# First attention of a two-layer kernel: scores from queries and keys of 64 channels, two heads side by side, stages of four heads

## The reference, cut to what matters

```python
H, D = 16, 64                                   # 8 batches, 256 queries, 1601 keys, 128 channels
q = (x @ Wq).reshape(B, S, H, D).transpose(0, 2, 1, 3)      # x: layer-normed tokens
k = (c @ Wk).reshape(B, N, D, H).transpose(0, 3, 2, 1)
v = (c @ Wv).reshape(B, N, D, H).transpose(0, 3, 1, 2)
mask = jnp.all(c == 0, axis=-1)[:, None, None, :]
scores = jnp.where(mask, -jnp.inf, jnp.einsum('bhsd,bhdn->bhsn', q, k) * D ** -0.5)
out = jnp.einsum('bhsn,bhnd->bhsd', jax.nn.softmax(scores, axis=-1), v)
return out.transpose(0, 2, 1, 3).reshape(B, S, H * D) @ Wo
```

## Time and profile before

| | |
|---|---|
| median of 3 runs | 2098.92 us (2096.93 to 2101.98) |
| profiled execution: time, span | 2103.45 us, 2101.7 us |
| PE busy, share of the span | 1975.8 us, 94% |
| DVE busy | 1674.0 us, 80% |
| ACT busy | 1071.4 us, 51% |
| POOL busy | 1196.0 us, 57% |
| first attention | from 0 to about 1576 us |

### The profile page before, as it was taken

The page is one execution under the profiler, slowest core; times in us unless marked ns, Lnnn a source line. Parts: engine busy times, 40 slices in busy tenths (PEclk is TensorE's granted clock), DMA queues, the critical chain, the costliest instruction groups (busy, mean ns, idle before and its releaser), DMA issues. The chain is left out here.

```text
span 2101.7 us, 35280 instructions
## 1 busy us (share of the span) xinstructions
PE 1975.8 (94%) x10757; PEld 1446.0 (69%) x10757; DVE 1674.0 (80%) x4067; ACT 1071.4 (51%) x1509; POOL 1196.0 (57%) x655
## 2 busy tenths in 40 slices
PE   7999999999999999999999999999987799769995
PEld 5667776777677777767777777777655588557774
DVE  7898888878788888888788888888656677757755
ACT  4444545354454545353544545454546699644442
POOL 5556575757466665757575665657666355223340
PEclk8999999999999999999999999999998999879997
DMA  3000000000000000000000000000000212112300
GB/s 97 1 8 10 2 3 17 1 1 4 18 1 4 17 1 1 3 18 1 4 1 17 1 4 6 1 1 1 6 1 21 82 64 77 37 47 63 87 24 24
DMA packets 56401, 40.81 MB, mean 19 GB/s; under 512 B 2516, under 2 KB 53660, under 8 KB 55196
## 3 DMA queue, kind: packets, MB, share of 16 engines
q1 hardware_dynamic: 56220, 38.57, 6.2%
HBM read 37.45 MB, written 1.11 MB: 18 GB/s over the span
## 5 line engine op out<-in xcount | busy, mean ns | idle before, releaser
L580 POOL TENSOR_TENSOR a_den<-a_den,a_probs 128x1024 f32<-128x1024 f32 x352 | 845.0, 2402 | 353.8 <-ACT a_probs L823 353.3
L823 ACT ACTIVATE a_probs<-a_probs,a_mask_col 128x1024 f32<-128x1024 f32 x416 | 478.9, 1151 | 576.6 <-DVE a_probs L1058 576.3
L1058 DVE TENSOR_TENSOR a_probs<-a_scores,a_shift 128x512 f32<-128x512 f32 x832 | 565.7, 686 | 150.5 <-PE a_scores L611 128.2
L957 DVE CUSTOM_DVE_ANT_0 a_work<-a_work,a_mask_row 128x400 f32<-128x400 f32 (+1 forms) x1024 | 572.5, 590 | 47.7 <-PE a_work L643 47.5
L711 PE MATMUL a_pv<-a_probs,a_V 128*64 128x256 f32 x3328 | 405.2, 385 | 0.9 <-ACT a_probs L823 0.9
L609 PE MATMUL a_scores<-a_Q_hi,a_cT_hi 128*128 128x512 f32 x832 | 346.0, 416 | 5.9 <-DVE a_probs L1058 4.4
L610 PE MATMUL a_scores<-a_Q_lo,a_cT_hi 128*128 128x512 f32 x832 | 328.5, 395 | 0.0
L643 PE MATMUL a_work<-a_cT_hi,a_Q_hi 128*128 128x400 f32 (+1 forms) x1024 | 327.1, 369 | 1.1 <-DVE a_Q_lo L910 0.4
L611 PE MATMUL a_scores<-a_Q_hi,a_cT_lo 128*128 128x512 f32 x832 | 327.2, 393 | 0.0
L711 PEld LDWEIGHTS a_pv<-a_probs,a_V 128*64 128x64 f32 x3328 | 220.4, 136 | 149.4 <-issue 40.2
L643 PEld LDWEIGHTS a_work<-a_cT_hi,a_Q_hi 128*128 128x128 f32 x1024 | 194.2, 190 | 97.0 <-issue 44.2
(11 more groups left out here) (357 smaller groups left out, 2833.8 us busy)
## 6 DMA issues: line engine op xcount, KB each, us to landing
m_gate_rows<-gate_scratch SPq DMA_DIRECT2D x8, 1024.0 KB, 4.6
a_c_nat<-in_ctx_dram SPq DMA_DIRECT2D x8, 768.0 KB
b_c_in<-in_ctx_dram SPq DMA_DIRECT2D x8, 768.0 KB
b_c_nat<-in_ctx_dram SPq DMA_DIRECT2D x8, 768.0 KB
m_w_raw<-in_L_ffn_W_dram SPq DMA_DIRECT2D x16, 256.0 KB, 5.0
a_acc<-in_x_dram SPq DMA_DIRECT2D x8, 128.0 KB, 2.1
out_dram<-tokens SPq DMA_DIRECT2D x4, 256.0 KB, 2.3
tokens<-in_x_dram SPq DMA_DIRECT2D x1, 896.0 KB, 9.3
```

The costliest lines, as they stand in the source:

```text
L580: nc.gpsimd.tensor_tensor(half, so_far, probs[:, buffer(c, j), :], ALU.add).then_inc(den_added, 1)
L823: nc.scalar.activation(probs[:, buffer(c, j), :], probs[:, buffer(c, j), :], ACT.Exp, bias=mask_col[:, c // 2 % 2, chunk:chunk + 1]).then_ ...
L957: nc.vector.tensor_tensor_reduce(out=X[:, bank, :w], in0=X[:, bank, :w], in1=mask_row[:, off:off + w], scale=1.0, scalar=-3e38, op0=ALU.ad ...
L1058: nc.vector.tensor_tensor(probs[:, buffer(c, j), pair * 2 * S:(pair + 1) * 2 * S], Sc[:, pair, :], shift[:, first:first + 2 * S], ALU.add) ...
```

## The change

The first attention is written anew; nothing else is touched, except that two new tiles of it lie where the experts' `m_xT` did.

- Queries and keys are made per pair of heads, with 64 channels a head: item `q` (one per stage, 2 x 3 matmuls) and new items `k` (eight per stage, each 3 matmuls of 400 to 462 columns). ACT copies a key piece's high part, DVE writes its low part.
- Even heads lie on rows 0 to 63, odd heads on rows 64 to 127. A score product is two matmuls of 64 rows, one on each half of the array, for 256 columns, into two PSUM banks. The same goes for `max`, which takes two banks of `a_work` at a time and is then reduced by two DVE operations.
- The shift is added on PE by one more pair of matmuls (`pick`, `shiftT`). DVE's subtraction is gone; ACT takes the exponential from PSUM into `a_probs`.
- A stage is one batch and four heads: 32 stages of 13 steps; a step is still four heads and one chunk of keys. There is one set of score banks, so scores wait for the exponential of the step before (`probs_done`).
- The order inside a step is now: scores of the next step, the `max` items, in every second step the two steps' `pv`, then the other items.

```diff
+            def scores(it, c, j):
+                if c > 0 or j > 0:
+                    pe.wait_ge(probs_done, steps_of(it, c, j))
+                if j == 0:
+                    all_taken(pe, it, made_before(c, ("q", "k", "spread")))
+                keys = slice(j * P, (j + 1) * P)
+                for p in range(PAIRS):
+                    queries = slice(p * S, (p + 1) * S)
+                    for n, (left, right) in enumerate(((0, 0), (0, 1), (1, 0))):
+                        for odd in range(2):
+                            rows = slice(HD * odd, HD * odd + HD)
+                            nc.tensor.matmul(Sc[:, odd, queries], K[c % 2][left][rows, p, keys],
+                                             Q[c % 2][right][rows, queries], start=(n == 0), stop=False)
+                    for odd in range(2):
+                        rows = slice(HD * odd, HD * odd + HD)
+                        last = nc.tensor.matmul(Sc[:, odd, queries], pick[rows, p, :], shiftT[rows, c % 2, :],
+                                                start=False, stop=True)
+                last.then_inc(scores_done, 1)
...
+            def maximum(it, s, m, use):
+                p, piece, half = m // 8, m // 2 % 4, m % 2
...
+                for odd in range(2):
+                    taken(pe, it, use + odd - BANKS)
+                for odd in range(2):
+                    rows = slice(HD * odd, HD * odd + HD)
+                    first = p * S + half * P
+                    nc.tensor.matmul(X[:, (use + odd) % BANKS, :w], Q[s % 2][0][rows, first:first + P],
+                                     K[s % 2][0][rows, p, off:off + w], start=True, stop=True)\
+                      .then_inc(bank_full[(use + odd) % BANKS], 1)
...
+            def body(it, c):
+                for j, slot in enumerate(plan(c)):
+                    if j + 1 < STEPS:
+                        scores(it, c, j + 1)
+                    elif has_next(it, c):
+                        scores(it, c + 1, 0)
+                    for s, kind, i, use in slot:
+                        if kind == "max":
+                            item(it, s, kind, i, use)
+                    if not wide(c, j):
+                        pv(it, *previous(c, j))
+                        pv(it, c, j)
+                    for s, kind, i, use in slot:
+                        if use is not None and kind != "max":
+                            item(it, s, kind, i, use)
...
             def exp(it, c, j):
-                act.wait_ge(shifted, shifts_of(it, c, j, 2))
...
-                nc.scalar.activation(probs[:, buffer(c, j), :], probs[:, buffer(c, j), :], ACT.Exp,
-                                     bias=mask_col[:, c // 2 % 2, chunk:chunk + 1]).then_inc(probs_done, 1)
+                act.wait_ge(scores_done, steps_of(it, c, j + 1))
...
+                nc.scalar.activation(probs[:, buffer(c, j), :].rearrange("p (o n) -> p o n", o=2), Sc[:, :, :], ACT.Exp,
+                                     bias=mask_col[:, c // GROUPS % 2, j:j + 1]).then_inc(probs_done, 1)
```

More of the change, by code:

```diff
@@ L250, in raw_plan @@
-        return slots
-    def raw_prologue():
-        items = [("cT", i) for i in range(3)] + [("cxT", 3), ("mask", 0), ("mask", 1), ("q", 0), ("q", 1),
-                                                 ("mask", 2), ("mask", 3)]
-        vs = [("v", i) for i in range(FIRST_VS)]
-        for m in range(32):
-            items.append(("max", m))
-            if m % 4 == 3 and m > 11:
-                items.append(vs.pop(0))
-        items += [("shift", 0), vs.pop(0), ("diag", 0), ("diag", 1), vs.pop(0), ("spread", 0), ("spread", 1)]
-        assert not vs
-        return [(-1, *item) for item in items]
+                others[6 + t // 3 if t < 8 else 9 + (t - 8) // 2].append((s, "scale", t))
@@ new lines, in raw_plan @@
+            for g, j in enumerate((8, 9, 11, 12)):
+                others[j].append((s, "mT", g))
+            for g, j in enumerate((9, 10, 12, 12)):
+                others[j].append((s, "ml", g))
+        return [a + b for a, b in zip(rows, others)]
+    def raw_prologue():
+        items = [(0, "cT", i) for i in range(3)] + [(0, "cxT", 3), (0, "q", 0)]
+        items += [(0, "flag", i) for i in range(4)] + [(0, "mask", i) for i in range(4)]
+        for i in range(KS):
+            items.append((0, "k", i))
+            if i > 0:
+                items += [(0, "max", 2 * i - 2), (0, "max", 2 * i - 1), (0, "v", i - 1)]
+        items += [(0, "max", MAXES - 2), (0, "max", MAXES - 1), (0, "shift", 0), (0, "spread", 0)]
+        return items
@@ L391, in taken, with all_taken @@
             eng.wait_ge(bank_free[use % BANKS], at(it, PER_TURN // BANKS, use // BANKS + 1))
+        def all_taken(eng, it, wanted):
+            for bank in range(BANKS):
+                of_bank = [use for use in wanted if use % BANKS == bank]
+                if of_bank:
+                    taken(eng, it, max(of_bank))
         def stages(eng, body):
-            body(None, 0)
+            for c in range(FIRST_TURN):
+                body(None, c)
             with eng.Fori(0, 3) as it:
-                for c in range(1, 5):
+                for c in range(FIRST_TURN, FIRST_TURN + TURN):
@@ L416, in the_plan @@
[L416 to L432 removed]
+            return at(it, TURN * STEPS, c * STEPS + first)
@@ L736, in _ @@
-            for _, kind, i, use in prologue_items()[:CONTEXT_ITEMS - 1]:
-                item(None, -1, kind, i, use)
-            pe.wait_ge(wT_copied, 2)
-            for g in range(H // 2):
-                for odd in range(2):
-                    rows = slice(HD * odd, HD * odd + HD)
-                    last = nc.tensor.matmul(setup_psum[odd][:, g * P:(g + 1) * P], wqT[rows, g * P:(g + 1) * P],
-                                            wkT[rows, g * P:(g + 1) * P], start=True, stop=True)
@@ new lines, in scores, with pv @@
+                last.then_inc(scores_done, 1)
+            def pv(it, c, j):
+                pe.wait_ge(probs_done, steps_of(it, c, j + 1))
+                if j == 0:
+                    if c > 1:
+                        pe.wait_ge(pv_free, at(it, TURN, c - 1))
+                    all_taken(pe, it, made_before(c, ("v",)))
+                for p in range(PAIRS):
+                    queries = slice(p * S, (p + 1) * S)
+                    for odd in range(2):
+                        h = 2 * p + odd
+                        first = odd * PAIRS * S + p * S
+                        last = nc.tensor.matmul(PV[HD * odd:HD * odd + HD, c % 2, queries],
+                                                V[:, c % 2, j, h * HD:(h + 1) * HD],
+                                                probs[:, buffer(c, j), first:first + S],
+                                                start=(j == 0 and p == 0), stop=(j == STEPS - 1), skip_group_check=True)
+                last.then_inc(pv_done, 1)
@@ L754, in _ @@
                 if use is not None:
-                    item(None, -1, kind, i, use)
-            for j in range(2):
-                for pair in range(2):
-                    qk(None, 0, j, pair)
+                    item(None, s, kind, i, use)
+            pe.wait_ge(pick_ready, 1)
+            scores(None, 0, 0)
             pe.wait_ge(wo_loaded, 16)
```

810 lines of the change are left out of this document (330 added, 480 removed).

## The result

The changed kernel takes **2181.84 us** (median of 4 runs, 2179.23 to 2186.96) against 2098.38 before (2096.93 to 2101.98): 1.0398 times as long, 95% interval 1.0375 to 1.0421, some 83 us slower. Forecast were 2135 us and a slowdown of 37. The side was right and the time lies in the range, but the loss is more than twice what was forecast.

The account below looks back on a forecast made before the run. PE was taken to bound the kernel at 94.9 us a stage. Work -9.8, shape changes +2.4 and waits +9.9 gave +2.5 us a pair, +36 in all: 2139 profiled, 2135 us as median, range 2045 to 2225.

Parts of the forecast that it names:

- PE's work, -9.8 us a pair: PE's matmul time in the attention falls by 9.8 us per two new stages, which replace one old stage.
- the terms of -11.4 and -5.7: PE gains per pair from running scores (11.4 us) and `max` (5.7 us) as couples on both array halves.
- The rival of a partial overlap: Array halves overlap only in part, couples wait for weight loads: 2370 us, halfway 2250; chance 0.15 for partial or none.
- Changes of shape, +2.4: Switching PE between row halves and full array costs 0.10 us each, 24 further changes a pair; bounds 0 and 4.8.
- C and D: A batch's third and fourth stages, from one normalisation to the next, preparing neither mask nor context; the pair walked.
- Waits, 12.0 against 2.1: PE's waits in the attention: 12.0 us per new pair against 2.1 per old stage, +9.9; bounds 5 and 16.
- Its third kind: A value or key item right behind two `max` waits for the first one's bank: 4.2 us a pair.
- its fourth: Scores wait for the shift on ACT and for an even stage's uncovered last exponential: 2.1 us a pair.
- the first two kinds: Second `max` waits for the last key piece's bank, 2.8 us a pair; third and fourth `max` wait for DVE, 2.9.
- The sum, +2.5 us a pair times 14: Work -9.8, changes of shape +2.4 and waits +9.9 make +2.5 us a pair, +35 over the 14 pairs.
- The faster rival: With 6 us of waits and free changes of shape a pair is 5.9 us shorter, 2017 us; chance 0.35.
- PE at 85 to 88%: Sign expected in the new profile: PE's busy share in the attention.

Follow-up runs that it names:

- number 6: Changed kernel with three extra single matmuls ahead of the bank wait of each third and later `max` item of a step; 2167.28 us.
- number 3: Changed kernel with the third and later `max` items of a step issued behind `pv` on PE; 2139.50 us.
- number 9: Changed kernel with DVE taking the context's low part for only 64 of each 512 columns, in every batch but the first; 2169.18 us.
- Numbers 4 and 5: On number 3: at most one `max` per wide step, three per narrow, 2088.53 us; then also the last value item in seven-wide-step stages' last step, 2080.22 us.
- number 7: Changed kernel with the even head's four score matmuls of a couple group issued first, then the odd head's, instead of alternating; 2219.91 us.
- number 11: Changed kernel with all eight score matmuls of a step's even heads issued first, then all eight of the odd heads; 2413.19 us.

## Why the prediction was right in its side and wrong in its size

**PE's work, -9.8 us a pair: holds as far as can be read.** The halves overlap in full. In PE's timeline the couples of scores start 0.12 apart and those of `max` take 0.18, which were the terms of -11.4 and -5.7. The rival of a partial overlap falls: a couple costs what a single matmul of as many columns does, 0.12 us for 256. With it falls the estimate of 0.154 us a couple that was worked out from the Trainium skill, page "TensorE: Matmul & The Clock Gate", Part 3, section Measured speedup vs the span model. (The rival's price without any overlap was added up too low: 24.5 + 5.8 make +30 us a pair on the work, and so some 33 over the old stage, not 28. Nothing hangs on it.)

**Changes of shape, +2.4: right in kind, too small.** PE's timeline has 51 of them in C and D (442.56 to 539.98) and 30 in a plain old stage (1132 to 1227), so 21 more. Each costs 0.09 us ahead of it and once more 0.09 behind the first matmul in the new shape, 0.18 in all where 0.10 was taken: up to +3.8 us, within the bounds.

**Waits, 12.0 against 2.1: nearly right for the pair that it walked.** From start to start, PE's timeline has some 10 us of waits in the same C and D. Its third kind comes to 4.1 us (4.2 forecast) and its fourth to 2.1 (2.1 forecast); the first two kinds were taken 1.4 us too high. The pair came out at 97.4 us, exactly the forecast, because waits taken too high and changes of shape taken too low cancel: the walk was good, the last digit is luck.

**The sum, +2.5 us a pair times 14: this is the step that failed, in two places.**

*It left the clock at 1.00.* The text named a clock that leaves 1.00 as what would make it wrong and gave it no term and no rival. The forecast's own second kind of wait, third and fourth `max` items behind DVE, brings about ten of the 14 falls, and its fourth kind the other four. The text spoke of up to four `max` items in one step; the last stage of each batch in the order has a step with five, and the clock fell there in all seven batches. The changed kernel loses 30.8 us to the clock, the kernel before 1.7, so some 29. Its own stages (1.6 to 1.8 us for 1.7 in D, 2.9 for 3.4) and number 6 (13.4 for 15.4) show that this is paid nearly in full, and number 3 that the ten falls go with those bursts.

*It took C and D for every pair.* The walked pair was set against the old mean of 94.9, in which the old kernel's context and masks are included. The kernel before, one batch (POOL's timeline):

```profile
655.67 2.40 POOL L548 TENSOR_TENSOR a_outT<-a_outT,a_rden 128x1024 f32<-128x1024 f32 x1
750.13 2.38 POOL L548 TENSOR_TENSOR a_outT<-a_outT,a_rden 128x1024 f32<-128x1024 f32 x1
845.45 2.40 POOL L548 TENSOR_TENSOR a_outT<-a_outT,a_rden 128x1024 f32<-128x1024 f32 x1
```

94.5 and 95.3: its two stages of a batch differ by 0.8 us. In the new order the two pairs of a batch differ by 2.0 (A and B 99.4, C and D 97.4, from number 6's batch without a fall). Context and mask items bring waits of their own, up to 1.1 us for a context's low part: number 9 takes 0.9 off A. The other 1.1 us stay open. The mean without falls is 98.4, 1.0 a pair above the walk: 14 us.

The account: 35 forecast + 14 for the unwalked pair + 29 for the clock = 78, and the 14 pairs are 80 longer. Only B's length without a fall (49.0) is taken from number 6; in the changed kernel, 50.7 with 1.7 us lost agrees with it. Two A's are 1.8 and 2.0 us longer than the others without a fall, as two stages of the kernel before are (96.9 in place of 95.3); why, no run tells.

**The faster rival, decided at 9.5 us of waits a pair, was right as a mechanism.** Numbers 4 and 5 have the change's matmuls with fewer waits, at 92.9 and 92.5 for C and D, and they are faster than the kernel before, by 0.6% and 0.9%. It is the place of a stage's 16 `max` items that makes the difference between +4.0% and -0.6%.

**What the new profile would show.** PE at 85 to 88%: it is 91% (548.58 of 600), a share that the lower clock raises, since matmuls last longer. Normalisation every 48.5 to 49 us: 50.3 on the mean. The sign that would make it wrong, the clock, was there.

## What to carry to other kernels

Work taken from the bounding engine pays only where nobody has to come back in time for what it used: here a faster `max` asked for its PSUM banks sooner than the engine behind could return them. A bank's round is mostly hand-over, so a faster reader helps less than another item in between; at most one two-bank item ahead of a full-array item, and the third of a burst behind a long group, was worth 93 us. When PE is forecast to pause several times in a row, put the clock into the sum: each fall cost 1.6 to 3 us here, some 28 in all. And walk every kind of stage of the period, not the plain one against the mean of all.

## What the runs showed of the hardware that I had not expected

- **One half of the array overtakes up to three matmuls of the other.** Blocks of four (number 7) still overlap and cost 0.07 us a step, blocks of eight overlap by half (number 11) and cost 0.5. Whether the three is a number of matmuls or something that scales with their length, no run here tells.
- **A change of shape is paid on both sides,** 0.09 us ahead of it and 0.09 behind the first matmul of the new shape, between 128x128, 64x128 and 128x64.
- **A tiny VectorE operation held up for 1.6 us.** The operation on 128x8 at line 908 takes 1613 ns on the mean, at least 173 and at most 2144, where its like in the kernel before had a median of 290. At 495.16 it lasted to 497.06, and POOL's addition that started at 494.67 ended at 497.04. So it is in the whole trace: 30 of its 32 times an addition of POOL was under way when it started, and it ended 0.03 us after that addition. The two times with none under way, it took 173 ns. In the kernel before it is the same (22 of 32 times under way, ending 0.03 us after; else 171 to 173 ns); there the addition had less of its time left. The Trainium skill, page "SBUF — State Buffer", section SBUF: two separate sides, says that VectorE operations of some kinds and GpSimd take turns at a shared pair of ports, one blocking the other for a whole instruction. Both traces agree in every place; no run took POOL's additions away to test it. Only once did PE wait for this operation.
- **The same waits need not bring a fall each time.** The step of D with four `max` items has the same order in all seven batches, and the clock fell there in three. Three single matmuls in each wait took away about half of the lost clock (number 6); a mere change of order took away every fall behind `max` items (number 3).
